# Graph-network kernel: TensorE sums gathered node rows in five more passes a chunk, two more counted rows, edge lists moved in two parts

## What is computed

```python
msg = x[src] + edge_attr
agg = segment_sum(msg, dst, 12500)
h = relu(agg @ W1 + b1)
out = layernorm(x + h @ W2 + b2)
```

## Time and profile before

| | us |
|---|---|
| median of three runs | 1507.69 |
| the profiled execution, its own time | 1504.08 |
| its span, first to last instruction | 1502.3 |
| start of the first slot's matrices | about 101 |
| start of slot 600 | 977 |
| last gather issued | 1407 |
| end of the last slot | 1413 |
| layers and normalisation | 1413 to 1502.3 |

### The profile page before, as it was taken

How to read it: one execution, slowest core, us unless ns; L and a number is a source line. 1 busy time by engine, 2 the same in 40 slices (tenths; PEclk the granted TensorE clock), 3 DMA queues, 4 the chain that set the end, 5 groups by cost and what they waited for, 6 DMA issues and landing times.

```text
span 1502.3 us, 43214 instructions
## 1 busy us (share of the span) xinstructions
PE 1212.9 (81%) x15541; PEld 979.2 (65%) x15542; DVE 1346.7 (90%) x3537; ACT 840.6 (56%) x1767; POOL 1076.9 (72%) x1139
## 2 busy tenths in 40 slices
PE   1235767778787887888888888899999999999895
PEld 1134656655666776776655555688888888888853
DVE  4659999999999899899999999999999999999644
ACT  1044444668435566567444444567777777766454
POOL 9758777777777777777777777777777777777312
PEclk8555578999999999999999999999999999999997
DMA  2833444444444444444444443444444444433133
GB/s 103 212 85 79 120 113 111 116 111 109 108 115 112 114 115 106 108 109 116 112 114 107 104 117 102 113 112 111 112 112 109 111 113 113 113 100 94 23 79 93
DMA packets 159272, 162.50 MB, mean 108 GB/s; under 512 B 53817, under 2 KB 141801, under 8 KB 158729
## 3 DMA queue, kind: packets, MB, share of 16 engines
q1 hardware_dynamic: 124679, 122.86, 27.9%
q0 software_dynamic: 34384, 36.90, 12.8%
HBM read 154.78 MB, written 4.85 MB: 106 GB/s over the span
## 4 chain that ended last, share of the span: by engine, by line
PE 31%; DVE 29%; issue 16%; POOL 11%; DVEq 4%; ACT 2%; DMA 1%; POOLq 0%; ACTq 0%
PE sums_ps L1092 12%; PE counted_ps L1076 11%; POOL xmsg L572 11%; DVE oh_key L878 10%; DVE oh_lo L874 6%; PE chunk_ps L1059 5%; DVE onehot L835 5%; DVE lists L856 3%; DVE gmsg L828 2%; DVEq L848 2%; PE turn_ps L1104 2%; ACT counts L674 1%; DVE less_b L788 1%; DVEq L856 1%; PE counted_ps L1160 1%
## 5 line engine op out<-in xcount | busy, mean ns | idle before, releaser
L572 POOL DMA_INDIRECT xmsg<-in_x,idx_t x1025 | 995.5, 971 | 322.4 <-issue 307.8
L674 ACT CAST counts<-counted_ps 128x392 bf16<-128x392 f32 (+2 forms) x1375 | 675.2, 545 | 480.6 <-PE counted_ps L1076 468.1
L1076 PE MATMUL counted_ps<-oh_key,oh_lo 128*128 128x196 bf16 (+3 forms) x4206 | 524.7, 255 | 123.2 <-DVE oh_key L878 105.9
L878 DVE TENSOR_TENSOR oh_key<-counted_ps,tables 128x980 bf16<-128x980 f16 (+4 forms) x883 | 541.3, 613 | 0.0
L1092 PE MATMUL sums_ps<-x_parts,counts 128*128 128x193 bf16 (+4 forms) x4410 | 495.0, 249 | 0.3
L1076 PEld LDWEIGHTS counted_ps<-oh_key,oh_lo 128*128 128x128 bf16 x4206 | 290.5, 102 | 227.3 <-DVE oh_key L878 167.0
L1092 PEld LDWEIGHTS sums_ps<-x_parts,counts 128*128 128x128 bf16 (+4 forms) x4410 | 396.3, 109 | 38.6 <-issue 1.9
L874 DVE TENSOR_TENSOR oh_lo<-counted_ps,tables 128x640 bf16<-128x640 f16 (+3 forms) x883 | 412.3, 467 | 9.9 <-PE counted_ps L1076 1.0
L1059 PE MATMUL chunk_ps<-onehot,cmsg 128*64 128x32 f32 (+1 forms) x4200 | 254.1, 231 | 26.2 <-DVE gmsg L828 23.6
L1059 PEld LDWEIGHTS chunk_ps<-onehot,cmsg 128*64 128x64 f32 x4200 | 220.1, 145 | 60.9 <-issue 43.2
L835 DVE TENSOR_TENSOR onehot<-counted_ps,rel_t 128x160 f32<-128x160 f32 (+1 forms) x625 | 234.3, 375 | 0.2
(11 more groups left out here) (96 smaller groups left out, 450.2 us busy)
## 6 DMA issues: line engine op xcount, KB each, us to landing
cmsg<-in_edge_attr SPq DMA_DIRECT2D x420, 160.0 KB
gmsg<-in_edge_attr SPq DMA_DIRECT2D x205, 160.0 KB
xmsg<-in_x,idx_t POOLq DMA_INDIRECT x1025
x_parts<-in_x SPq DMA_DIRECT2D x12, 256.0 KB, 3.4
out_nodes<-x_parts SPq DMA_DIRECT2D x12, 256.0 KB, 2.6
edge_records<-counts SPq DMA_DIRECT2D x1, 1575.0 KB
lists<-in_src SPq DMA_DIRECT2D x1, 1562.5 KB
lists<-in_dst SPq DMA_DIRECT2D x1, 1562.5 KB
```

What stands on the lines that cost most here:

```text
L572: pool.indirect_dma_start(xmsg[:, at * D:(at + 1) * D], None, x, bass.IndirectOffsetOnAxis(ap=idx_t[:, of:of + 1], axis=0)).then_inc(gathe ...
L674: nc.scalar.copy(to, ps.rearrange("p (n h) -> p h n", h=HI)).then_inc(unit_kept, 1)
L878: nc.vector.tensor_tensor(oh_key[s % RING][:, 0:n * w].rearrange("p (k n o) -> p k n o", k=n, o=2), key_ps[:, 0:w].rearrange("p (n o) -> p ...
L1076: mm = nc.tensor.matmul(unit_ps[u % BANKS][:, col:col + slot.key_cols], oh_lo[s % RING][:, n * P:(n + 1) * P], oh_key[s % RING][:, n * slo ...
```

## The change

- `products` runs ten passes for a gathered chunk, five with the edge features and five with the gathered rows as the stationary operand, against the same 0/1 matrix, all into one PSUM sum. `mix` and the semaphore `mixed` are gone. TensorE itself waits for the edge load and the gathers; GpSimd's buffer of chunk k is free when the pair of chunk k is summed.
- `summed` is raised for both chunks of a pair by the pair's last matmul.
- `CROWS` is 86: 430 counted chunks and 195 gathered ones.
- The planner's gathered chunk takes 6.45 us.
- DMAs that span 125, 84 or now 86 partitions are two: the largest multiple of 16 partitions, and the rest.

```diff
-CROWS = 84
+CROWS = 86
+def in_sixteens(rows):
+    return (0, rows // 16 * 16), (rows // 16 * 16, rows)
...
-    FIRST, LAST = 90.0, 36.0 + 6.6 * gathered + 1.4 * groups
+    FIRST, LAST = 90.0, 36.0 + 6.45 * gathered + 1.4 * groups
...
-            sp.dma_start(src_i, src_v).then_inc(src_in, 16)
-            sp.dma_start(dst_i, dst_v).then_inc(dst_in, 16)
+            for to, of, done in ((src_i, src_v, src_in), (dst_i, dst_v, dst_in)):
+                for a, b in in_sixteens(ROWS):
+                    sp.dma_start(to[a:b, :], of[a:b, :]).then_inc(done, 16)
...
-            sp.dma_start(most_dram.rearrange("(t k) -> t k", t=CROWS), most[0:CROWS, :]).then_inc(most_out, 16)
+            for a, b in in_sixteens(CROWS):
+                sp.dma_start(most_dram[a * FINES:b * FINES].rearrange("(t k) -> t k", k=FINES), most[a:b, :]).then_inc(most_out, 16)
...
-            sp.dma_start(record_dram[0:CFINE, :].rearrange("(t b) k -> t (b k)", t=CROWS),
-                         counts[0][0:CROWS, 0:FINES * REC].bitcast(i16)).then_inc(records_out, 16)
+            for a, b in in_sixteens(CROWS):
+                sp.dma_start(record_dram[a * FINES:b * FINES, :].rearrange("(t b) k -> t (b k)", b=FINES),
+                             counts[0][a:b, 0:FINES * REC].bitcast(i16)).then_inc(records_out, 16)
...
-                    pool.wait_ge(mixed, k - XSLOTS + 1)
+                    pool.wait_ge(summed, PLACE["gather", k - XSLOTS] + 1)
...
-            def mix(k):
-                s, t = k % GSLOTS, k % XSLOTS
-                dve.wait_ge(gin[s], 16 * (k // GSLOTS + 1))
-                dve.wait_ge(gathered[t], 16 * TILES * (k // XSLOTS + 1))
-                to = gmsg[:, s * TILES * D:(s + 1) * TILES * D]
-                nc.vector.tensor_tensor(to, to, xmsg[:, t * TILES * D:(t + 1) * TILES * D], ALU.add).then_inc(mixed, 1)
...
-                    if kind == "gather":
-                        mix(i)
...
-                    return cmsg[:, s * TILES * D:(s + 1) * TILES * D]
-                s = i % GSLOTS
-                pe.wait_ge(mixed, i + 1)
-                return gmsg[:, s * TILES * D:(s + 1) * TILES * D]
+                    return [cmsg[:, s * TILES * D:(s + 1) * TILES * D]]
+                s, t = i % GSLOTS, i % XSLOTS
+                pe.wait_ge(gin[s], 16 * (i // GSLOTS + 1))
+                pe.wait_ge(gathered[t], 16 * TILES * (i // XSLOTS + 1))
+                return [gmsg[:, s * TILES * D:(s + 1) * TILES * D], xmsg[:, t * TILES * D:(t + 1) * TILES * D]]
...
-                for j in range(TILES):
+                steps = [[(of, j) for of in parts for j in range(TILES)] for parts in rows]
+                for n in range(max(len(x) for x in steps)):
                     for half, (place, kind, i) in enumerate(pair):
-                        w = width_of(kind, i)
-                        mm = nc.tensor.matmul(chunk_ps[place // 2 % 2][half * D:(half + 1) * D, 0:w], rows[half][:, j * D:(j + 1) * D],
-                                              onehot[place % OSLOTS][:, j * w:(j + 1) * w], start=(j == 0),
-                                              stop=(j == TILES - 1))
-                        if j == TILES - 1:
-                            mm.then_inc(summed, 1)
+                        if n < len(steps[half]):
+                            (of, j), w = steps[half][n], width_of(kind, i)
+                            mm = nc.tensor.matmul(chunk_ps[place // 2 % 2][half * D:(half + 1) * D, 0:w], of[:, j * D:(j + 1) * D],
+                                                  onehot[place % OSLOTS][:, j * w:(j + 1) * w], start=(n == 0),
+                                                  stop=(n + 1 == len(steps[half])))
+                mm.then_inc(summed, len(pair))
```

More of the change, by code:

```diff
@@ L364, in build @@
         gathered = [sem(f"gathered{s}") for s in range(XSLOTS)]
-        mixed = sem("mixed")
         marked, summed, added = sem("marked"), sem("summed"), sem("added")
@@ L464, in _ @@
             sp.wait_ge(most_made, 1)
-            sp.dma_start(most_dram.rearrange("(t k) -> t k", t=CROWS), most[0:CROWS, :]).then_inc(most_out, 16)
+            for a, b in in_sixteens(CROWS):
+                sp.dma_start(most_dram[a * FINES:b * FINES].rearrange("(t k) -> t k", k=FINES), most[a:b, :]).then_inc(most_out, 16)
             sp.wait_ge(records_made, 2)
-            sp.dma_start(record_dram[0:CFINE, :].rearrange("(t b) k -> t (b k)", t=CROWS),
-                         counts[0][0:CROWS, 0:FINES * REC].bitcast(i16)).then_inc(records_out, 16)
-            sp.wait_ge(most_out, 16)
+            for a, b in in_sixteens(CROWS):
+                sp.dma_start(record_dram[a * FINES:b * FINES, :].rearrange("(t b) k -> t (b k)", b=FINES),
+                             counts[0][a:b, 0:FINES * REC].bitcast(i16)).then_inc(records_out, 16)
+            sp.wait_ge(most_out, 32)
             for g in range(EARLY_GROUPS):
@@ L577, in load_records @@
                 pool.wait_ge(run_ready, g + 1)
-                pool.wait_ge(records_out, 32)
+                pool.wait_ge(records_out, 48)
                 if g >= 2:
@@ L625, in _ @@
         def _(act):
-            act.wait_ge(src_in, 16)
+            act.wait_ge(src_in, 32)
             nc.scalar.copy(src_f, src_i).then_inc(src_copied, 1)
@@ L665, in keep_unit @@
                     if unit.block == 0:
-                        act.wait_ge(records_out, 32)
+                        act.wait_ge(records_out, 48)
                     elif unit.block == 1:
@@ L750, in _ @@
             fine = lambda a: a.rearrange("t (b e) -> t b e", e=FINE)
-            dve.wait_ge(src_in, 16)
+            dve.wait_ge(src_in, 32)
             link(nc.vector.tensor_scalar(hi_i[0:CROWS, :], src_i[0:CROWS, :], LOG_P, None, ALU.arith_shift_right))
@@ L755, in _ @@
                                            op0=ALU.mult, op1=ALU.add).then_inc(records_made, 1)
-            dve.wait_ge(dst_in, 16)
+            dve.wait_ge(dst_in, 32)
             nc.vector.tensor_reduce(most[:, :], fine(dst_i), axis=AX.X, op=ALU.max).then_inc(most_made, 1)
```

## The result

The changed kernel takes **1532.13 us** (median of 3 runs, 1532.09 to 1532.15) against 1507.69: a ratio of 1.0165 [1.0141, 1.0188], 1.65% slower. Forecast were 1516.5 us, in a range of 1505 to 1535: the sign is right, the size, +8.8 us for +24.4 us, is not. The profiled execution took 1532.09 us with a span of 1530.3.

The account below looks back on a forecast made before the run. GpSimd and VectorE bound slots before 600, all three engines later. Slot 600 at 913 us plus TensorE's 508 us ends the slots at 1421 us for 1413; 1507.7 + 8.8 = 1516.5 us, range 1505 to 1535 us.

Parts of the forecast that it names:

- Ten passes for five, 0.58 us a chunk: TensorE: five added passes per gathered chunk cost 0.58 us; 113 us for 195 chunks, 74 before slot 600, 39 after.
- Rival 3: TensorE weight loads don't overlap matmuls: 2.0 us a chunk, about 1750 us in all; chance 0.02.
- From slot 600 TensorE sets the pace, 508 us: Slots from 600 on: TensorE's time, 436 - 8 + 35 + 6 + 39 = 508 us.
- Rival 1: From slot 600 TensorE isn't full and GpSimd sets the pace: under 496 us there, 1444 to 1488 in all; chance 0.24.
- 86 rows: 28 more slots at the list's end, 50 gathers fewer: TensorE 35 us more late, GpSimd 62 us less.
- Lists in two parts, at nothing: Start: edge lists land sooner, but VectorE's wait for `most_b` grows by what they save; priced at nothing.
- rival 4: The start comes forward by up to 15 us if `most_b` isn't the last wait: 1502 us; chance 0.04.
- Slots 0 to 599 go at GpSimd's pace: Before slot 600: 53 fewer gathers at 1.27 us save 67 us; slot 600 starts at 913 us, not 977.
- Rival 2: Slots before 600 don't speed up, longer pairs delay VectorE: a third on its path 1541 us, all 1590; chance 0.17.
- GpSimd's pace doesn't depend on: Removing `mix` takes 82 to 98 us off VectorE but leaves GpSimd's pace and TensorE's late pace unchanged.
- The start: GpSimd's first buffer wait lasts about 2 us longer, added DMA issues on SyncE's queue cost 1 us.
- Signs: Expected in the trace: GpSimd without waits to slot 600, then about 60 us for TensorE's pairs; last slot near 1421 us.

Follow-up runs that it names:

- Passes alone: Kernel before with `mix` taken out and ten passes, but 84 rows and every transfer in one part: 1522.9 us, ratio 1.0111.
- rows alone: Changed kernel with `mix` back on VectorE and five passes; 86 rows and transfers in two parts stay: 1536.58 us, ratio 1.0223.
- the like pairs: Changed kernel with chunks paired like with like, two gathered or two counted in a pair: 1559.12 us, ratio 1.0349.
- the last experiments above: Several of the same kernels run on three chips where the kernel before took 2523 to 2556 us; ten passes with 84 rows: 2450.82 us, ratio 0.9594.

## Why the prediction was right, and where it failed

- **Ten passes for five, 0.58 us a chunk**: right. Loads of `xmsg` are 58 ns apart, and late a chunk's passes are worth 0.53 us. Rival 3 falls: the 1950 loads of `xmsg` take 145 ns each and start 58 ns apart. The Trainium skill's rule ("TensorE: Matmul & The Clock Gate", Part 3, "The mechanism"; the prediction names the section behind it), that a load overlaps a running matmul only in another row group, does not hold for these loads.
- **From slot 600 TensorE sets the pace, 508 us**: right, 508.7. Its terms stand singly too: without the passes 472.7 (469 by the sum), with 84 rows 465.6 (466). Rival 1, under 496 us, falls.
- **86 rows**: right in its counts; 35 us for 28 slots fits the 472.7 us without the passes. With `mix` TensorE's sum gives 469 us and the stretch took 476.8, VectorE's work at 96%.
- **Lists in two parts, at nothing**: right; rival 4 falls.
- **"Slots 0 to 599 go at GpSimd's pace"**: this step failed. From 300 to 599 it should have given 28 us and gave 15. GpSimd's own work there did fall by 29 us (331 to 302), but its waits for VectorE's search rose from 5.7 to 20.2 us. I had seen that VectorE would be "a tie" and that TensorE "fits" into its waits, and took the tie as if the slower engine set the time. The runs show three engines with 300 to 303 us of work taking 321.7, and 302.8 when VectorE and TensorE are both relieved. Rival 2 named this ("three engines above 93% disturb each other") and put the whole at a third of 127 x 0.58 = 25 us; 13 to 16 us were lost at slot 600. Its first half, pairs that hold VectorE up, is worth at most the 6.0 us that came back without the passes, and its sign, slot 600 after 940 us, did not come. I gave it 0.17, and should have put part of it into the forecast.
- **Slots 0 to 299**: the number held, 38.3 us less against 31 x 1.27 = 39 us, in part by luck. "GpSimd's pace doesn't depend on" `mix` was wrong: without it the gathers of this stretch are 5 us shorter in all. The waits before GpSimd's record fetches, 4.6 us before and 12.4 after, took as much back. The granted clock rose too, from 0.87 to 0.93, but without the passes it was 0.90 and the stretch shorter, 496.3 us, so the clock does not set it by itself.
- **The start**: 2 + 1 us forecast, 5.6 measured. GpSimd's first buffer came free at 90.56 us and not at 87.01 + 2. Passes alone and rows alone each start slot 0 at 105.4 us, 3.7 late; what in each makes it was not taken apart, and this cause stays open.
- **The tail**, 89.3 us forecast, took 92.8. In all kernels the last part, from the hidden layer on, varies between 73 and 78 us; no cause was sought.
- **Signs**: "GpSimd without waits up to slot 600" was wrong, and the 72 us it waits late (about 60 in all were forecast) are for VectorE's search, not for TensorE's pairs. The slack was seen, its place in the order was not. TensorE's late waits for VectorE's matrices fell as forecast, at its weight loads from 10.3 to 4.6 us. The last slot ended at 1437.5 us, not near 1421.

In all: start 2.6, slots 0 to 299 1, slots 300 to 599 some 13, tail 3.5 us more than the sum, which gives the missing 19 to 20 us of the span (1510.6 to 1530.3). The median lies 0 to 4 us off the profiled execution, before 3.6 above, after equal.

## What to carry to other kernels

Cut the span where the bound changes and price a moved operation in each stretch: the same five passes cost 36 us where TensorE was full and 6 us where it had room, so the move paid only in the first part, and splitting it at slot 600 beats both kernels. Where a sum brings two engines that wait for each other to within a few per cent, the time need not be the larger of the two; here three with 300 to 303 us of work took 321.7. An operation moved off one engine can also change another's: without `mix`, GpSimd's gathers got shorter. And time saved on one engine (the like pairs) is a gain only if the result doesn't arrive later for whoever waits for it.

## What was unexpected of the hardware

In the last experiments above, TensorE stops with nothing that it waits for, in every kernel, before the matmuls of slots and chunks for 12 to 24 us at the longest, depending on the kernel; the mean granted clock is 0.74 to 0.77, where the same kernels have 0.91 to 0.94 above; and the order of two kernels turns round: the passes alone are 4% faster than the kernel before there and 1% slower elsewhere. A verdict holds for the condition in which it was measured. What the condition is, and whether the clock follows from the stops, was not found; it is no fixed property of a chip, as one of the three took 1507.88 us for the kernel before in another run.
